# Turning the retrieved rows by VectorE and sixteen SBUF moves instead of by TensorE, and centring by VectorE

## Chip, cores and metric

The kernel runs on one core of a Trainium2 chip. The metric is the device time of one execution in microseconds (us), the median over several runs. Engines are called PE (TensorE), DVE (VectorE), ACT (ScalarE), POOL (GpSimd) and SP (SyncE, which here only issues DMAs).

## What is computed

The input has 2048 rows of 512 numbers. Each row is normalised; from it an attention retrieval over 8 selected heads of 128 and a dense layer with int8 weights are computed, and both are added to the row. The key and value projections only feed outputs that are dropped.

```python
xn = _layernorm(x, axis=-1)
q = xn @ Wq.T + bq                      # heads of 128; only heads 0, 4, 8, ... (8 of 32) are used
sig_q = jax.nn.elu(q) + 1.0
num = jnp.einsum('bshd,hde->bshe', q_sel, M)
den = jnp.einsum('bshd,hd->bsh', q_sel, z)[..., None] + EPS
retrieved = num / den                   # repeated for the 4 heads of a group
output = retrieved_heads @ Wo.T
dense = xn @ (w * w_scale) + b
x = x + output + dense
```

## The kernel before

The 2048 rows are 16 tiles of 128 (t = 0 to 15). M and Wo are folded once into a matrix P (8 pieces of 128x512, line 740), so that per tile three products are left: q = centred x times Wq (`product_q`, two halves of 512 columns, 24 matmuls), the dense product (`product_dense`, 12 matmuls) and a times P (`product_attn`, 24 matmuls). Each product is made of three passes over operands split into a high and a low part (`three_passes`, lines 677 to 679); so every operand exists as `_hi` (a rounding copy, mostly by ACT) and `_lo` (the rest, by DVE).

Per tile the way is: DVE takes the moments (lines 462, 466, 470). PE spreads the mean over the partitions with one transpose into `mean_ps` (line 687); ACT copies it to `mean_b` (line 324), and POOL subtracts it from the transposed tile `xT` (`center`, line 225); for tiles 0 and 1 DVE does this from `mean_ps` (lines 480, 487). ACT and DVE split `xT` (lines 339, 500). PE makes q in PSUM; DVE scales and adds the bias (`add_bias`, 531); ACT makes exp of the negative part (362, 364), DVE makes s = elu(q) + 1 (`make_s`, 538). POOL multiplies s by z (`times_z`, 256), DVE sums by head, adds the epsilon, takes the reciprocal (`denominator`, 543, 546, 550), ACT scales s by it, head by head, in place (`make_a`, 375): this is a, rows by heads. PE turns a with 8 transposes of 128x128 (`transpose_a`, 752) into two banks `aT_ps`; ACT and DVE split these into `aT_hi` and `aT_lo` (383, 563). Then `product_attn`, and DVE adds it to x (`add_attn`, 570; for the last tile line 671 in two halves).

The order of each engine is written out by hand; each engine works its list in order, and waits on semaphores. Tiles 0 to 6 are interleaved by hand with the loading of the weights and the making of P (by DMAs that POOL issues with addition, line 245, for the sum over the 4 head groups of Wo). Then a loop over t = 7 to 15 (LEAD = 7) does on PE: q(t), dense(t), spread of mean t+2, attn(t-7), turn of a(t-5). After the loop come attn(9) to attn(15) alone, with the remaining turns. DVE's body of the loop is: split of aT(t-6), bias, moments of t+2, bias, s, split of xT(t+1), s, dense added, denominator(t-4) (BEHIND = 4), attn(t-7) added. Eight PSUM banks: two for q, one dense, two aT, two attn, one mean; in tiles 0 to 6 q also uses the attn and aT banks. SP issues loads of x and xT, and the stores of finished tiles, each as one DMA of 128 partitions.

## Time and profile before

| | us |
|---|---|
| median of 3 runs | 260.02 |
| lowest, highest | 259.87, 264.77 |
| the profiled execution, its own time | 260.27 |
| its span in the trace (first to last instruction) | 258.5 |

The profile is one execution seen by the hardware profiler. The span leaves out what lies around the first and last instruction: 260.27 - 258.5 = 1.77 us. The granted TensorE clock is full in the whole span. A row that says "[1.21 <-DVE x L554]" means that the engine was idle 1.21 us before this instruction, until that line of DVE was done. Matmuls overlap in the rows: one takes 0.39 us from start to modelled end, but the next starts 0.23 us after it.

### The profile page before, as it was taken

Reading aid. Unit: us, or ns where it says so; the run is one execution under the profiler, and the core shown is the slowest. Engines: PE = TensorE matmul, PEld = TensorE weight load, DVE = VectorE, ACT = ScalarE, POOL = GpSimd, SP = SyncE. Lnnn points to the kernel's source line nnn. Section 1 sums busy time; section 2 is a strip of 40 time slices with the busy share of each in tenths; the row PEclk is TensorE's granted clock in tenths of the full one; section 3 lists DMA queues with packets and bytes.
Section 4 is the critical chain, followed back from the end, with each engine's and each line's share of the span. In section 5 each row is a group of like instructions: output and inputs, shape, how many; then the busy total and the mean of one; then the engine's idle time right before and its main releaser. Section 6 shows DMA issues by size and latency. Waiting matters only on the chain.

```text
span 258.5 us, 3387 instructions
## 1 busy us (share of the span) xinstructions
PE 249.9 (97%) x1156; PEld 201.2 (78%) x1156; DVE 156.2 (60%) x262; ACT 121.2 (47%) x276; POOL 103.2 (40%) x96
## 2 busy tenths in 40 slices
PE   6899899899998999999999999999999999999996
PEld 4477687687766888888888888888888888888885
DVE  4849996898677846457483746557463445555321
ACT  3653625657457554444345553544345345555100
POOL 2594745580303670705235070714305055563000
PEclk9999999999999999999999999999999999999999
DMA  7999999995400003030302103010101001111111
GB/s 247 414 411 406 345 228 218 209 217 153 146 16 4 0 13 109 0 124 1 122 1 66 58 0 122 3 41 0 41 3 41 1 1 43 41 41 43 49 49 64
DMA packets 9808, 26.42 MB, mean 102 GB/s; under 512 B 1088, under 2 KB 1344, under 8 KB 8640
## 3 DMA queue, kind: packets, MB, share of 16 engines
q1 hardware_dynamic: 8640, 19.40, 20.2%
q0 software_dynamic: 864, 6.29, 11.8%
q10 hardware_dynamic: 288, 0.52, 0.6%
q8 instruction: 9, 0.15, 0.2%
q14 instruction: 7, 0.06, 0.1%
HBM read 22.02 MB, written 4.19 MB: 101 GB/s over the span
## 4 chain that ended last, share of the span: by engine, by line
PE 84%; DVE 9%; ACT 2%; issue 2%; DMA 1%; DVEq 0%
PE attn_ps L679 11%; PE attn_ps L677 11%; PE attn_ps L678 11%; PE q_ps L677 8%; PE q_ps L679 8%; PE q_ps L678 8%; PE aT_ps L752 5%; PE dense_ps L677 5%; PE dense_ps L678 5%; PE dense_ps L679 5%; PE attn_ps L740 2%; DMA x<-in_x 1%; DVE stats L462 1%; DVE wd_lo L517 1%; DVE q_ps L531 1%
## 5 line engine op out<-in xcount | busy, mean ns | idle before, releaser
L256 POOL TENSOR_TENSOR e_and_sz<-s,z_b 128x512 f32<-128x512 f32 x32 | 41.7, 1330 | 31.4 <-DVE den L543 31.4
L375 ACT ACTIVATE s<-s,rden 128x128 f32<-128x128 f32 x128 | 39.2, 389 | 31.0 <-DVE rden L550 31.0
L677 PE MATMUL attn_ps<-P_hi,aT_hi 128*128 128x512 f32 (+1 forms) x128 | 50.2, 393 | 0.0
L679 PE MATMUL attn_ps<-P_hi,aT_lo 128*128 128x512 f32 (+1 forms) x128 | 49.2, 385 | 0.0
L678 PE MATMUL attn_ps<-P_lo,aT_hi 128*128 128x512 f32 (+1 forms) x128 | 49.0, 382 | 0.0
L570 DVE TENSOR_TENSOR x<-attn_ps,x 128x512 f32<-128x512 f32 x15 | 10.4, 691 | 46.4 <-PE attn_ps L679 46.4
L677 PE MATMUL q_ps<-WqT_hi,xT_hi 128*128 128x512 f32 x88 | 36.0, 409 | 0.6 <-DVE s L538 0.6
L679 PE MATMUL q_ps<-WqT_hi,xT_lo 128*128 128x512 f32 x88 | 34.4, 391 | 0.0
L678 PE MATMUL q_ps<-WqT_lo,xT_hi 128*128 128x512 f32 x88 | 34.3, 390 | 0.0
L219 POOL TENSOR_TENSOR rstd<-vareps,neg_half 128x1 f32<-128x1 f32 x16 | 10.6, 665 | 55.7 <-DVE vareps L470 55.7
L225 POOL TENSOR_TENSOR xT<-xT,mean_b 128x512 f32<-128x512 f32 x14 | 19.6, 1403 | 32.5 <-ACT mean_b L324 32.5
L531 DVE SCALAR_TENSOR_TENSOR q_ps<-q_ps,rstd,bq_b 128x512 f32<-128x512 f32 x24 | 18.1, 758 | 21.5 <-PE q_ps L679 21.5
L362 ACT ACTIVATE e_and_sz<-q_ps 128x512 f32<-128x512 f32 x24 | 14.3, 596 | 33.9 <-DVE q_ps L531 33.9
L679 PEld LDWEIGHTS attn_ps<-P_hi,aT_lo 128*128 128x128 f32 x128 | 24.1, 188 | 4.9
L677 PEld LDWEIGHTS attn_ps<-P_hi,aT_hi 128*128 128x128 f32 x128 | 24.1, 188 | 4.9
L678 PEld LDWEIGHTS attn_ps<-P_lo,aT_hi 128*128 128x128 f32 x128 | 24.1, 188 | 4.4
L677 PE MATMUL dense_ps<-wd_hi,xT_hi 128*128 128x512 f32 x64 | 25.6, 400 | 1.2 <-DVE x L554 1.2
L383 ACT ACTIVATE aT_hi<-aT_ps 128x512 fp32r<-128x512 f32 x32 | 17.4, 595 | 17.0 <-PE aT_ps L752 17.0
L679 PE MATMUL dense_ps<-wd_hi,xT_lo 128*128 128x512 f32 x64 | 24.9, 390 | 0.0
L678 PE MATMUL dense_ps<-wd_lo,xT_hi 128*128 128x512 f32 x64 | 24.9, 390 | 0.0
L563 DVE TENSOR_TENSOR aT_lo<-aT_ps,aT_hi 128x512 fp32r<-128x512 f32 x32 | 20.6, 685 | 5.2 <-ACT aT_hi L383 5.2
L364 ACT ACTIVATE e_and_sz<-e_and_sz 128x512 f32<-128x512 f32 x32 | 20.2, 632 | 1.0
(93 smaller groups left out, 407.9 us busy)
## 6 DMA issues: line engine op xcount, KB each, us to landing
x<-in_WoT POOLq DMA_DIRECT2D x6, 1024.0 KB, 9.6
x<-in_x SPq DMA_DIRECT2D x16, 256.0 KB, 3.7
xT<-in_xT SPq DMA_DIRECT2D x16, 256.0 KB, 4.1
out<-x SPq DMA_DIRECT2D x15, 256.0 KB, 2.0
x<-in_WoT SPq DMA_DIRECT2D x2, 1024.0 KB, 14.6
s<-in_WqT SPq DMA_DIRECT2D x3, 512.0 KB, 7.0
s<-in_w_scale SPq DMA_DIRECT2D x1, 1024.0 KB, 10.1
s<-in_WqT ACTq DMA_DIRECT2D x2, 256.0 KB, 4.2
```

The lines of the kernel that those rows point to most:

```text
L225: nc.gpsimd.tensor_tensor(xT[:, t % XRING, :, :], xT[:, t % XRING, :, :], mean_b[:, t % 2, :].unsqueeze(1).to_broadcast([P, K, P]), ALU.su ...
L256: nc.gpsimd.tensor_tensor(szbuf[:, halves(h)], sbuf_s[:, t % SRING, halves(h)], z_b[:, halves(h)], ALU.mult).then_inc(sz_ready, 1)
L362: nc.scalar.activation(e, q_bank(t, h)[:], ACT.Relu, scale=-1.0).then_inc(qneg_ready, 1)
L364: nc.scalar.activation(e, e, ACT.Exp, scale=-1.0).then_inc(exp_ready, 1)
L375: last = nc.scalar.activation(a_g, a_g, ACT.Copy, scale=rden[:, t % 2, g:g + 1])
L383: nc.scalar.activation(aT_hi[:, t % 2, h * GH:(h + 1) * GH, :].rearrange("p g r -> p (g r)"), aT_ps[h][:], ACT.Copy).then_inc(aT_hi_ready, 1)
L531: nc.vector.scalar_tensor_tensor(q_bank(t, h)[:], q_bank(t, h)[:], rstd[:, t:t + 1], bq_b[:, halves(h)], ALU.mult, ALU.add).then_inc(q_bia ...
L563: nc.vector.tensor_tensor(aT_lo[:, t % 2, gs, :].rearrange("p g r -> p (g r)"), aT_ps[h][:], aT_hi[:, t % 2, gs, :].rearrange("p g r -> p ...
L677: nc.tensor.matmul(out, x_hi, w_hi, start=start, stop=False)
L678: nc.tensor.matmul(out, x_hi, w_lo, start=False, stop=False)
L679: return nc.tensor.matmul(out, x_lo, w_hi, start=False, stop=stop)
L752: last = nc.tensor.transpose(aT_ps[h][:, i * P:(i + 1) * P], sbuf_s[:, t % SRING, g * D:(g + 1) * D], ident[:])
```

## The change

- PE no longer turns a. Instead DVE transposes the tile of a in place, in blocks of 32x32 (`turn_blocks`, one instruction on 128x1024), and SP moves the blocks with 16 DMAs of 32 partitions by 1 KB, SBUF to SBUF (`spread_blocks`), into `aT` for even tiles and into the space of `MT` (free once P is made) for odd ones. To make runs of 1 KB, the columns of Wq, bq and z are laid out by quarters of a head (32 columns of each head together); `times_z`, `make_a` and the splits read and write with views over four pieces of 32.
- DVE centres every tile from `mean_ps`; `copy_mean` on ACT and `center` on POOL are gone.
- The epsilon of the denominator is a 129th column that is summed with the others; the addition on DVE (line 546) is gone.
- The two banks of aT become a second pair of q banks; q(t) waits for s(t-2) instead of s(t-1).
- BEHIND is 3 instead of 4, the ring of s has 6 places instead of 7, and the lists of all engines are reordered to match. `spread_blocks(t)` waits for `turn_blocks(t)` and for the split of aT(t-2); `copy_aT_hi(t)` waits for all 16 DMAs; `make_s(t, 0)` waits for the DMAs of tile t-6.
- On PE 14 filling matmuls in bf16, 8 before and 6 after the first spread mean, replace 7 in fp32r and 5 in bf16; on SP the load of the second piece of Wq goes before that of x(1).

```diff
-    SRING = 7
+    SRING = 6
     XRING = 4
     HRING = 4
-    BEHIND = 4
+    BEHIND = 3
...
         sbuf_s = sb("s", [P, SRING, E])
-        e_and_sz = sb("e_and_sz", [P, 2, E])
+        aT = sb("aT", [P, 4, E // 4])
+        e_and_sz = sb("e_and_sz", [P, E + G * (D + 1)])
         aT_hi = sb("aT_hi", [P, 2, G, P], F32R)
         aT_lo = sb("aT_lo", [P, 2, G, P], F32R)
-        w_words = sb("w_words", [P, K, HID // 4], I32)
-        mean_b = sb("mean_b", [P, 2, P])
...
-        warm_b = sb("warm_b", [P, HID], BF16)
-
-        warm_r = P_hi[:, 0, :]
-        w_i8 = w_words[:].bitcast(I8)
+        warm = sb("warm", [P, P], BF16)
+
+        w_words = aT[:, 0:2, :].rearrange("p a (k w) -> p (a k) w", k=K // 2).bitcast(I32)
...
-        szbuf = e_and_sz[:, 1, :]
-        w_f32 = e_and_sz[:].rearrange("p r (a n) -> p (r a) n", n=HID)
+        ebuf = e_and_sz[:, 0:E]
+        sz_eps = e_and_sz[:, E:].rearrange("p (g d) -> p g d", g=G)
...
-        q_ps = [bank("q0_ps"), bank("q1_ps")]
+        q_ps = [bank(f"q{i}_ps") for i in range(4)]
         dense_ps = bank("dense_ps")
-        aT_ps = [bank("aT0_ps"), bank("aT1_ps")]
         attn_ps = [bank("attn0_ps"), bank("attn1_ps")]
         mean_ps = bank("mean_ps")
 
         def q_bank(t, h):
-            return ([q_ps, attn_ps, aT_ps][t % 3] if t < LEAD else q_ps)[h]
+            if t < LEAD and t % 3 == 1:
+                return attn_ps[h]
+            return q_ps[2 * (t % 3 == 2 if t < LEAD else t % 2) + h]
...
+        def by_quarter(v):
+            return v.rearrange("p (j g c) -> p j g c", g=G, c=D // 4)
+
+        def aT_place(t):
+            return [aT[:], MT[:].rearrange("p g d -> p (g d)").rearrange("p (i e) -> p i e", i=4)][t % 2]
+
+        def by_head(t, gs):
+            return aT_place(t).rearrange("p i (g r) -> p g i r", g=G)[:, gs]
+
+        def in_groups(v):
+            return v.rearrange("p g (i r) -> p g i r", i=4)
+
+        def aT_landed(t):
+            return 16 * 16 * (t // 2 + 1)
...
+            def spread_blocks(t):
+                sp.wait_ge(a_turned, t + 1)
+                if t == 1:
+                    sp.wait_ge(P_filled, G)
+                elif t >= 2:
+                    sp.wait_ge(aT_lo_ready, 2 * t - 2)
+                for i in range(4):
+                    for j in range(4):
+                        sp.dma_start(aT_place(t)[j * 32:(j + 1) * 32, i, :],
+                                     sbuf_s[i * 32:(i + 1) * 32, t % SRING, j * E // 4:(j + 1) * E // 4]
+                                     ).then_inc(aT_in[t % 2], 16)
...
-            for t in range(5, T):
-                if t >= FIRST_LENT:
-                    sp.wait_ge(P_filled, t - FIRST_LENT + 1)
+            for t in range(5, FIRST_LENT):
                 load_x(t)
                 load_xT(t)
-                if t >= 10:
-                    sp.wait_ge(attn_added, t - 9)
-                    sp.dma_start(out_d[t - 10], x[:, t - 10, :]).then_inc(stored, 16)
-            for t in range(T - 10, T - 1):
-                sp.wait_ge(attn_added, t + 1)
-                sp.dma_start(out_d[t], x[:, t, :]).then_inc(stored, 16)
+            spread_blocks(0)
+            for t in range(FIRST_LENT, LEAD + 4):
+                sp.wait_ge(P_filled, t - FIRST_LENT + 1)
+                load_x(t)
+                load_xT(t)
+            spread_blocks(1)
+            spread_blocks(2)
+            for t in range(LEAD, T):
+                if t + 4 < T:
+                    sp.wait_ge(P_filled, t + 4 - FIRST_LENT + 1)
+                    load_x(t + 4)
+                    load_xT(t + 4)
+                spread_blocks(t - BEHIND - 1)
+                if t - LEAD >= 1:
+                    store(t - LEAD - 1)
+            for t in range(T - BEHIND - 1, T):
+                spread_blocks(t)
+                store(t - BEHIND - 1)
+            for t in range(T - BEHIND - 1, T - 1):
+                store(t)
...
-            def center(t):
-                pool.wait_ge(mean_copied, t - 1)
-                pool.wait_ge(xT_in[t], 16)
-                nc.gpsimd.tensor_tensor(xT[:, t % XRING, :, :], xT[:, t % XRING, :, :],
-                                        mean_b[:, t % 2, :].unsqueeze(1).to_broadcast([P, K, P]), ALU.subtract
-                                        ).then_inc(xc_by_pool, 1)
...
-                nc.gpsimd.tensor_tensor(szbuf[:, halves(h)], sbuf_s[:, t % SRING, halves(h)],
-                                        z_b[:, halves(h)], ALU.mult).then_inc(sz_ready, 1)
+                nc.gpsimd.tensor_tensor(sz_eps[:, :, h * D // 2:(h + 1) * D // 2].rearrange("p g (j c) -> p j g c", j=2),
+                                        by_quarter(sbuf_s[:, t % SRING, halves(h)]), by_quarter(z_b[:, halves(h)]), ALU.mult
+                                        ).then_inc(sz_ready, 1)
...
-            def copy_mean(t):
-                act.wait_ge(mean_filled, t + 1)
-                if t >= 4:
-                    act.wait_ge(xc_by_pool, t - 3)
-                nc.scalar.activation(mean_b[:, t % 2, :], mean_ps[:, 0:P], ACT.Copy
-                                     ).then_inc(mean_copied, 1)
...
-                    a_g = sbuf_s[:, t % SRING, g * D:(g + 1) * D]
+                    a_g = by_quarter(sbuf_s[:, t % SRING, :])[:, :, g, :]
                     last = nc.scalar.activation(a_g, a_g, ACT.Copy, scale=rden[:, t % 2, g:g + 1])
                 last.then_inc(a_ready, 1)
 
             def copy_aT_hi(t):
+                act.wait_ge(aT_in[t % 2], aT_landed(t))
+                if t >= 2:
+                    act.wait_ge(attn_filled, t - 1)
                 for h in range(2):
-                    act.wait_ge(aT_filled, 2 * t + h + 1)
-                    if t >= 2:
-                        act.wait_ge(attn_filled, t - 1)
-                    nc.scalar.activation(aT_hi[:, t % 2, h * GH:(h + 1) * GH, :].rearrange("p g r -> p (g r)"),
-                                         aT_ps[h][:], ACT.Copy).then_inc(aT_hi_ready, 1)
+                    gs = slice(h * GH, (h + 1) * GH)
+                    nc.scalar.activation(in_groups(aT_hi[:, t % 2, gs, :]), by_head(t, gs), ACT.Copy).then_inc(aT_hi_ready, 1)
...
+            make_a(3)
             for t in range(LEAD, T):
-                copy_aT_hi(t - LEAD + 1)
                 exp_of(t, 0)
                 if t + 1 < T:
                     copy_xT_hi(t + 1)
                 exp_of(t, 1)
-                if t + 2 < T:
-                    copy_mean(t + 2)
+                copy_aT_hi(t - LEAD + 1)
                 make_a(t - BEHIND)
             for t in range(T - LEAD + 1, T):
                 copy_aT_hi(t)
-                if t + 2 < T:
-                    make_a(t + 2)
+                if t + BEHIND < T:
+                    make_a(t + BEHIND)
...
-            def center_second():
-                dve.wait_ge(mean_filled, 2)
-                dve.wait_ge(xT_in[1], 16)
-                nc.vector.tensor_tensor(xT[:, 1, :, :], xT[:, 1, :, :],
+            def center(t):
+                dve.wait_ge(mean_filled, t + 1)
+                dve.wait_ge(xT_in[t], 16)
+                nc.vector.tensor_tensor(xT[:, t % XRING, :, :], xT[:, t % XRING, :, :],
                                         mean_ps[:, 0:P].unsqueeze(1).to_broadcast([P, K, P]),
                                         ALU.subtract).then_inc(xc_by_dve, 1)
...
-                    dve.wait_ge(aT_filled, 2 * (t - SRING) + 2)
+                    dve.wait_ge(aT_in[(t - SRING) % 2], aT_landed(t - SRING))
...
-                nc.vector.reduce_sum(den[:], szbuf.rearrange("p (g d) -> p g d", g=G), AX.X
-                                     ).then_inc(den_ready, 1)
+                nc.vector.reduce_sum(den[:, t % 2, :], sz_eps, AX.X).then_inc(den_ready, 1)
                 dve.wait_ge(den_ready, t + 1)
-                nc.vector.tensor_scalar_add(den_e[:], den[:], DEN_EPS).then_inc(den_e_ready, 1)
-                dve.wait_ge(den_e_ready, t + 1)
                 if t >= 2:
                     dve.wait_ge(a_ready, t - 1)
-                nc.vector.reciprocal(rden[:, t % 2, :], den_e[:]).then_inc(rden_ready, 1)
+                nc.vector.reciprocal(rden[:, t % 2, :], den[:, t % 2, :]).then_inc(rden_ready, 1)
...
+            def turn_blocks(t):
+                dve.wait_ge(a_ready, t + 1)
+                nc.vector.transpose(sbuf_s[:, t % SRING, :], sbuf_s[:, t % SRING, :]).then_inc(a_turned, 1)
...
-                    nc.vector.tensor_tensor(aT_lo[:, t % 2, gs, :].rearrange("p g r -> p (g r)"), aT_ps[h][:],
-                                            aT_hi[:, t % 2, gs, :].rearrange("p g r -> p (g r)").bitcast(F32),
-                                            ALU.subtract).then_inc(aT_lo_ready, 1)
+                    nc.vector.tensor_tensor(in_groups(aT_lo[:, t % 2, gs, :]), by_head(t, gs),
+                                            in_groups(aT_hi[:, t % 2, gs, :]).bitcast(F32), ALU.subtract
+                                            ).then_inc(aT_lo_ready, 1)
...
+            center(3)
...
+            center(8)
+            turn_blocks(2)
             for t in range(LEAD, T):
-                split_aT_lo(t - LEAD + 1)
                 add_bias(t, 0)
                 if t + 2 < T:
                     moments(t + 2)
                 add_bias(t, 1)
+                turn_blocks(t - BEHIND - 1)
                 make_s(t, 0)
                 if t + 1 < T:
                     split_xT_lo(t + 1)
                 make_s(t, 1)
+                split_aT_lo(t - LEAD + 1)
                 add_dense(t)
+                if t + 2 < T:
+                    center(t + 2)
                 denominator(t - BEHIND)
+                if t == T - 1:
+                    denominator(T - BEHIND)
                 add_attn(t - LEAD)
             for t in range(T - LEAD, T - 1):
                 split_aT_lo(t + 1)
-                if t + 3 < T:
-                    denominator(t + 3)
+                if t + BEHIND < T:
+                    turn_blocks(t + BEHIND)
+                if t + BEHIND + 2 < T:
+                    denominator(t + BEHIND + 2)
                 add_attn(t)
             for c in range(2):
...
-                if 1 <= t <= 2:
+                if t >= 1:
                     pe.wait_ge(xc_by_dve, t + 1)
-                elif t >= 3:
-                    pe.wait_ge(mean_copied, t - 2)
...
-                    pe.wait_ge(s_ready, 2 * (t - 3 if t < LEAD else t - 1) + h + 1)
+                    pe.wait_ge(s_ready, 2 * (t - 3 if t < LEAD else t - 2) + h + 1)
...
-            def transpose_a(t):
-                pe.wait_ge(a_ready, t + 1)
-                for h in range(2):
-                    if t == 0:
-                        pe.wait_ge(s_ready, 11 + h)
-                    else:
-                        pe.wait_ge(aT_lo_ready, 2 * t - 1 + h)
-                    for i in range(GH):
-                        g = h * GH + i
-                        last = nc.tensor.transpose(aT_ps[h][:, i * P:(i + 1) * P],
-                                                   sbuf_s[:, t % SRING, g * D:(g + 1) * D], ident[:])
-                    last.then_inc(aT_filled, 1)
...
-            pe.wait_ge(warm_set, 2)
-            for i in range(3):
-                nc.tensor.matmul(dense_ps[:], warm_r[:, 0:P], warm_r, start=True, stop=True)
-            for i in range(4):
-                nc.tensor.matmul(aT_ps[i % 2][:], warm_r[:, 0:P], warm_r, start=True, stop=True)
+            def keep_busy(n):
+                for i in range(n):
+                    nc.tensor.matmul(dense_ps[:], warm[:], warm[:].unsqueeze(1).to_broadcast([P, 4, P]), start=True, stop=True)
+
+            pe.wait_ge(warm_set, 1)
+            keep_busy(8)
             pe.wait_ge(consts_set, 3)
             spread_mean(0)
-            for i in range(5):
-                nc.tensor.matmul(dense_ps[:], warm_b[:, 0:P], warm_b[:], start=True, stop=True)
+            keep_busy(6)
...
-            transpose_a(0)
...
-                transpose_a(t - LEAD + 2)
             for t in range(T - LEAD, T - 1):
                 product_attn(t)
-                if t + 2 < T:
-                    transpose_a(t + 2)
```

## Rows read from the trace of the kernel before

**Rows 1.** The page: each engine's busy time, share of the span, instructions.
```profile
PE 249.9 (97%) x1156; PEld 201.2 (78%) x1156; DVE 156.2 (60%) x262; ACT 121.2 (47%) x276; POOL 103.2 (40%) x96
```

**Rows 2.** The page: the chain that ended last, shares by engine.
```profile
PE 84%; DVE 9%; ACT 2%; issue 2%; DMA 1%; DVEq 0%
```

**Rows 3.** Chain in order of time: start us, us, what; end of P, turns.
```profile
75.04 0.87 PE attn_ps L740 x2
...
75.94 0.61 ACT P_hi L368
...
76.56 0.69 DVE P_lo L522
77.26 1.19 DVE aT_lo L563 x2
...
79.19 1.10 PE attn_ps L740 x2
80.29 0.87 PE aT_ps L752 x8
...
81.28 0.23 PE q_ps L677
...
212.05 0.88 PE aT_ps L752 x8
```

**Rows 4.** Timeline of PE and ACT, tiles 2 to 5: start, us, what, idle before.
```profile
31.12 0.47 PE L677 MATMUL q_ps<-WqT_hi,xT_hi 128*128 128x512 f32 x1 [0.55 <-DVE s L538]
...
46.37 0.50 PE L677 MATMUL dense_ps<-wd_hi,xT_hi 128*128 128x512 f32 x1 [1.21 <-DVE x L554]
...
39.72 0.28 ACT L324 ACTIVATE mean_b<-mean_ps 128x128 f32<-128x128 f32 x1 [5.66 <-PE mean_ps L687]
```

**Rows 5.** Groups by line: busy us, mean ns of one, idle before.
```profile
L543 DVE TENSOR_REDUCE den<-e_and_sz 128x8 f32<-128x1024 f32 x16 | 19.3, 1209 | 0.0
L546 DVE TENSOR_SCALAR den_e<-den 128x8 f32<-128x8 f32 x16 | 5.8, 361 | 0.6
L487 DVE TENSOR_TENSOR xT<-xT,mean_ps 128x512 f32<-128x512 f32 x1 | 0.7, 675 | 0.0
L517 DVE TENSOR_TENSOR wd_lo<-s,wd_hi 128x1024 fp32r<-128x1024 f32 x2 | 3.4, 1762 | 0.0
```

**Rows 6.** Stretches of one loop pass: busy us by engine, clock, DMA share, GB/s.
```profile
110.60:125.20 14.60, 14.60 (x71) 12.10 (x70) 8.49 (x15) 6.75 (x17) 5.63 (x5) 1.00 0.17 56
```

**Rows 7.** Timelines of SP's queue: start us, us, issue.
```profile
2.12 0.43 SPq L170 DMA_DIRECT2D s<-in_WqT  x1
2.59 0.43 SPq L167 DMA_DIRECT2D xT<-in_xT  x1
...
15.60 2.34 SPq L162 DMA_DIRECT2D x<-in_x  x1
...
61.31 0.33 SPq L162 DMA_DIRECT2D x<-in_x  x1
61.68 0.43 SPq L167 DMA_DIRECT2D xT<-in_xT  x1
```

**Rows 8.** DMA issues: KB each, us from issue to landing.
```profile
out<-x SPq DMA_DIRECT2D x15, 256.0 KB, 2.0
out<-x SPq DMA_DIRECT2D x2, 128.0 KB, 1.7
```

**Rows 9.** Timelines of DVE and POOL: subtraction alone, and beside POOL's product.
```profile
12.52 0.69 DVE L500 TENSOR_TENSOR xT_lo<-xT,xT_hi 128x512 fp32r<-128x512 f32 x1
...
18.70 2.53 DVE L500 TENSOR_TENSOR xT_lo<-xT,xT_hi 128x512 fp32r<-128x512 f32 x1 [3.77 <-ACT xT_hi L339]
...
18.29 2.39 POOL L237 TENSOR_TENSOR s<-e_and_sz,s 128x1024 f32<-128x1024 f32 x1 [0.43 <-ACT e_and_sz L349]
```

**Rows 10.** Timelines of the last loop pass and the end: ACT, DVE, POOL.
```profile
205.35 0.63 ACT L364 ACTIVATE e_and_sz<-e_and_sz 128x512 f32<-128x512 f32 x1
...
212.53 1.09 ACT L383 ACTIVATE aT_hi<-aT_ps 128x512 fp32r<-128x512 f32 x2 [0.85 <-PE aT_ps L752]
...
213.16 1.29 DVE L563 TENSOR_TENSOR aT_lo<-aT_ps,aT_hi 128x512 fp32r<-128x512 f32 x2 [0.38 <-ACT aT_hi L383]
...
250.18 0.69 DVE L570 TENSOR_TENSOR x<-attn_ps,x 128x512 f32<-128x512 f32 x1 [3.97 <-PE attn_ps L679]
...
208.60 2.54 POOL L256 TENSOR_TENSOR e_and_sz<-s,z_b 128x512 f32<-128x512 f32 x2 [10.71 <-DVE den L543]
```

More of the change, by code:

```diff
@@ L143, in retrieval_and_dense @@
         dense_added = sem("dense_added")
-        aT_filled = sem("aT_filled")
+        a_turned = sem("a_turned")
+        aT_in = [sem(f"aT_in{i}") for i in range(2)]
         aT_hi_ready = sem("aT_hi_ready")
@@ L248, in times_z @@
             def times_z(t, h):
-                if t == 0 and h == 0:
+                if t == 0:
                     pool.wait_ge(z_in, 16)
-                if t == 0:
-                    pool.wait_ge(wd_by_pool, 1)
+                    pool.wait_ge(eps_set, 1)
                 else:
@@ L313, in _ @@
                 times_z(t, 1)
-                add_b(t - BEHIND + 2)
-            for t in range(T - 2, T):
+                add_b(t - 3)
+            for t in range(T - 3, T):
                 add_b(t)
@@ L621, in _ @@
             add_bias(4, 1)
+            center(6)
             denominator(1)
+            turn_blocks(0)
             make_s(4, 0)
@@ L639, in _ @@
             split_P_lo(3)
+            denominator(3)
             split_xT_lo(7)
@@ L876 @@
         "xT": tiles.reshape(16, 128, 4, 128).transpose(0, 3, 2, 1).reshape(16, 128, 512),
-        "WqT": np.asarray(inputs["L0_attn_Wq"]).reshape(8, 4, 128, 4, 128).transpose(1, 3, 4, 0, 2).reshape(
+        "WqT": np.asarray(inputs["L0_attn_Wq"]).reshape(8, 4, 4, 32, 4, 128).transpose(1, 4, 5, 2, 0, 3).reshape(
             4, 4, 128, 1024),
-        "bq": np.asarray(inputs["L0_attn_bq"]).reshape(8, 4, 128)[:, 0].reshape(1024),
+        "bq": np.asarray(inputs["L0_attn_bq"]).reshape(8, 4, 4, 32)[:, 0].transpose(1, 0, 2).reshape(1024),
         "WoT": np.asarray(inputs["L0_attn_Wo"]).reshape(512, 2, 4, 4, 128).transpose(3, 1, 4, 2, 0).reshape(
@@ L882 @@
         "MT": np.asarray(inputs["L0_attn_M"]).transpose(2, 0, 1),
-        "z": np.asarray(inputs["L0_attn_z"]),
+        "z": np.asarray(inputs["L0_attn_z"]).reshape(8, 4, 32).transpose(1, 0, 2).reshape(1024),
         "w": np.ascontiguousarray(np.asarray(inputs["L0_ffn_w"]).reshape(4, 128, 512).transpose(1, 0, 2)).view(np.int32),
```

62 lines of the change are left out of this document (25 added, 37 removed).

## The prediction

> **What bounds the kernel now.** I read four views in this order. The page's first part: PE is busy in 97% of the span, DVE in 60, ACT in 47, POOL in 40 [rows 1]; the clock is full in the loop [rows 6]. The chain that ended last says the same more strictly: 84% of it is PE [rows 2]. Then the chain in order of time, for what PE does in a tile: the 8 turns of a stand in it with 0.88 us [rows 3], 16 times. So a microsecond taken from PE's list is worth a microsecond, as long as no other engine's list becomes the longer. Last, the timelines of tiles 2 to 6 and of the end, where PE does wait: 0.55 us for s at 31.12, 1.21 us for the dense sum at 46.37 [rows 4]. A loop pass from q to attn is 13.6 us without turns: from 81.28 to 212.05 there are nine passes and eight turns, (130.8 - 7.0) / 9 = 13.75 with the spread mean in most [rows 3].
>
> **PE loses the turns.** 16 x 0.87 = 13.9 us of list. The first two stand in the stretch where P is made. There a chain of product, copy 0.61, subtraction 0.69, split of aT(0) 1.19, subtraction, last product and the moments of tile 8 goes on without them. From the product at 75.04 to q of tile 7 at 81.28 it is 6.24 us; by that chain about 5.6 remain, a gain of 0.6 in place of 1.7 [rows 3]. The other 14 give 12.2.
>
> **Centring moves to DVE.** ACT loses the copy of the mean, POOL a product-sized instruction, DVE gets 0.68 per tile [rows 5], 14 tiles. In the loop DVE is busy 8.49 of 14.60 us [rows 6]; that becomes 8.5 + 0.7 + 1.2 (turn, below) - 0.2 = 10.2 of 13.7. Hidden. In tiles 2 to 5 DVE itself is on the chain, so each added 0.68 could cost. But there ACT stood 5.66 us in front of the mean of tile 5 [rows 4] with the exp of tile 2 behind it in its list, and two subtractions ran against POOL (1.76 us each where 1.2 is the size of a reduction over as many elements [rows 5]). Both go. Walking DVE's new list through, s(0) comes about 1.0 us earlier, so q of tile 3 starts about 0.9 earlier and dense of tile 1 about 0.8; the exp of tile 2 no longer waits, and add_dense(2) ends near 43.5 where PE comes to dense(3) at 44.3 instead of 46.37. I take 2.1 us gained; if the added work eats it, 0; these are the bounds.
>
> **The epsilon column.** The addition averages 361 ns where the reciprocal beside it is shorter, since it gets caught behind POOL [rows 5]. Gone, off PE's path: no term of its own. Two more q banks relax a wait that cost PE nothing in the loop: nothing. The new filling on PE ends about 0.4 us later before the first q, where PE then waits for weights anyway: nothing, up to 0.5 lost.
>
> **DVE's turn of 128x1024.** No row shows it. Nearest is the reduction over 128x1024, 1.21 us [rows 5]; as a lower bound 0.7, as an upper one twice the reduction, 2.4. I take 1.2. The Trainium skill ("VectorE: DVE Perf Modes", The three transpose paths) gives 311 ns for a 128x128 bf16 turn of this kind, which for eight would be an estimate of 2.5 us and put the sum below 1.3 us higher.
>
> **SP's sixteen moves per tile** are the term that takes back. DMAs issued in a row on SP start 0.47 us apart (2.12, 2.59), whatever their size; the shortest is 0.33, 0.37 to the next (61.31, 61.68) [rows 7]. Landing is 1.7 to 2.0 us after the issue [rows 8]. I take 0.47 and 2.0: a tile is 7.5 us of issue, plus a store. In the loop that is 19 issues, 8.9 of 13.7 us. spread_blocks(t) holds behind it on SP the next loads, needed two passes later, and a store; copy_aT_hi, which waits for the landing, comes a pass later; make_s(7, 0), which waits for tile 1's moves (they must wait for the end of P), may hold DVE a microsecond where PE has five in hand. So the loop runs on PE.
>
> At the end it doesn't. Call E the end of attn(8); attn(9) to attn(15) take 5.48 us each without turns (from 212.05 + 0.88 to 250.18, six products and five turns [rows 3, 10]), so attn(15) could start at E + 32.9. SP has four tiles of moves and three stores before it. In the last pass tile 11's moves wait for the split of aT(9), which now stands behind s(15, 1): by [rows 10] the exp ends 7.6 us into the pass, the split near 9.9, that is E - 3.7. Moves of 11 and a store end at E + 4.3. Tile 12's wait for its turn: DVE has before it denominator(13), which needs POOL's product of 2.54 us started behind denominator(12), then add_attn(8) and the split of aT(10). This gives E + 5.3. The split now has both inputs in SBUF; such a subtraction took 0.69 alone and 2.53 beside POOL [rows 9], so up to E + 7.1; I take E + 6. The last issue starts 66 issues later (4 x 16 + 3 stores, less one), lands after 2.0, half a copy and half a split (0.55 and 0.7 [rows 10]) follow: attn(15) at E + 6 + 66 x 0.47 + 2.0 + 1.25 = E + 40.3. Stall 7.4 us, spread over attn(13) to attn(15).
>
> **Sum.** E was at 212.05; less 2.1, 0.6 and 8 loop turns of 0.87 (7.0) it is 202.35. Plus 40.3, plus 8.3 from attn(15) to the end of the span (250.18 to 258.5), plus 1.77 outside it: 252.7 us against 260.27 of the profiled execution. The median is 0.25 under that: 252.4.
>
> **The rivals.**
> 1. *The moves are issued faster.* At 0.37 apart and a turn at E + 5.3 the stall is gone: 202.35 + 32.9 + 8.3 + 1.77 = 245.3, 245.1 as a median. For it: the shortest issue; against it: 0.43 and 0.47 in every row of several issues [rows 7].
> 2. *The end costs more or the start gives nothing.* With no early gain (+2.1), the split of aT(10) fully behind POOL (+1.1) and a slow turn (+1.2): 256.8. Each tenth of a microsecond on the issue is 6.6 us, so 0.53 apart gives 256.4 alone.
> 3. *Slower: small moves hold the queue.* If each DMA holds SP as long as one did with a full queue, 2.34 us [rows 7], 19 per pass are 44 us and the kernel is beyond 500. It decides from 0.59 apart (the sum passes 260.3) and from 13.7 / 19 = 0.72 SP bounds the loop as well; at 0.8 nine passes of 15.2 add another 13 us to the end's 22: about 288. For it: the long issues exist; against it: they lie where the DMA engines are full, and in the loop their share is 0.17 [rows 6]. The Trainium skill ("DMA: Bandwidth & Descriptors", Bandwidth) warns that transfers under 64 KB are dominated by descriptors and asks for 1 MiB or more; these have 32 KB. No row of before shows one of that size.
> 4. *DVE becomes the bound*: it needs a turn of 1.2 + (13.7 - 10.2) = 4.7 us, four times the reduction.
>
> **How the numbers follow.** My forecast 0.50 (its own range 249.5 to 254.8), rival 1 with all between 0.37 and 0.43 apart 0.22, rival 2 0.18, rival 3 0.07, rival 4 0.03. The predicted time is 252.4. The range reaches down to rival 1 and up past rival 2: 245.0 to 258.5. About 2% is what a measurement here can tell from no change: under 254.8 is faster, over 265.2 slower. The forecast lies under that line in nine of ten of its cases, rival 1 always, a tenth of rival 2: 0.45 + 0.22 + 0.02 = 0.69. Slower takes most of rivals 3 and 4: 0.08. The rest is 0.23.
>
> **What would show it.** DVE's turn near 1.2 us; SP's moves 0.47 apart, and 256 of them; no idle on PE in the loop, a pass of 13.7 us; dense(3) starting near 44; then PE waiting for the split of aT in front of attn(13), attn(14) and attn(15), about 7 us together, with SP's queue never idle from E on. If PE doesn't wait there, the moves are cheaper than I take them; if it waits inside the loop, they or the turn are dearer. What makes the forecast wrong first is the price of an issue, the factor 66 in the sum.

## The result and the profile after

The kernel after takes 277.9 us (median of 4 runs, 276.06 to 278.19) where the kernel before takes 260.0: a ratio of 1.0675, interval 1.0617 to 1.0733. The forecast was 252.4, with 245.0 to 258.5 as its range. It is slower, outside the range and on the other side. The profiled execution is 278.12 us with a span of 276.5.

The page of after: each engine's busy time, the granted clock over the span in 40 slices, and the chain that ended last by engine and by line.

```profile
PE 247.3 (89%) x1030; PEld 193.0 (70%) x1030; DVE 178.7 (65%) x275; ACT 117.9 (43%) x262; POOL 86.3 (31%) x83
...
PEclk9999995799999999999999999999999998959959
...
PE 58%; SPq 22%; DMA 10%; DVE 4%; issue 4%; ACT 1%
SPq L197 17%; DMA x<-in_x 9%; PE q_ps L708 8%; PE q_ps L706 8%; PE q_ps L707 8%; PE attn_ps L706 7%; PE attn_ps L707 7%; PE attn_ps L708 7%; PE dense_ps L706 4%; PE dense_ps L708 4%; PE dense_ps L707 4%; PE attn_ps L767 2%; SPq L180 1%; SPq L175 1%; DVE s L549 1%
```

Beside [rows 1] PE lost 126 instructions but only 2.6 us of busy time, because the clock is no longer full: it falls in two places, near 50 us and in the last fifth. Beside [rows 2] PE's share of the chain falls from 84 to 58%. Two newcomers took its place: SP issuing the moves (L197) and one load of x. PE's waits, summed by line (total us, times, longest), give each newcomer a size.

```profile
PE attn_ps L706 <- DVE aT_lo L575: 14.1, 4, 5.4
PE dense_ps L706 <- DVE x L562: 5.1, 1, 5.1
```

**The start.** q of tile 7 begins at 88.86 where it was 81.28 [rows 3]: 7.6 us lost. The chain in order of time (start, us, what) shows why:

```profile
13.46 25.97 DMA x<-in_x
...
39.46 0.70 DVE stats L473
```

PE's timeline has the wait that comes of it, and the windows (columns as in [rows 6]) what the clock was afterwards:

```profile
45.82 0.80 PE L706 MATMUL dense_ps<-wd_hi,xT_hi 128*128 128x512 f32 x1 [5.08 <-DVE x L562]
```
```profile
45.80:51.70 5.90, 5.88 (x14) 4.63 (x15) 5.04 (x10) 4.16 (x9) 1.83 (x3) 0.50 1.04 215
```

x of tile 5 is issued at 13.46 and lands at 39.43. DVE stands 6.3 us in front of its moments, everything behind them on DVE stands too, PE waits 5.1 us for the dense sum, and then runs 5.9 us at a granted clock of 0.50, the lower of its two levels. What changed around this load is on POOL: the adding transfers of Wo start 5 us earlier. POOL's timeline of before:

```profile
24.84 2.18 POOL L225 TENSOR_TENSOR xT<-xT,mean_b 128x512 f32<-128x512 f32 x1 [0.84 <-ACT mean_b L324]
26.98 1.92 POOL L245 DMA_DIRECT2D x<-in_WoT  x2
```

And that of after:

```profile
21.52 0.55 POOL L259 TENSOR_TENSOR rstd<-vareps,neg_half 128x1 f32<-128x1 f32 x1 [3.21 <-DVE vareps L481]
22.02 1.02 POOL L278 DMA_DIRECT2D x<-in_WoT  x1
23.57 0.86 POOL L278 DMA_DIRECT2D x<-in_WoT  x1 [0.53 <-DMA x<-in_WoT]
```

The centring of tile 3 used to stand in front of them in POOL's list: with its wait it took 3.0 us there (from 24.0 to 27.0). It is gone. The other 1.9 us are DVE's: POOL's instruction before it, which needs the moments of tile 3, starts at 21.52 where it started at 23.46, since DVE reaches these moments at 20.35 instead of 22.29. Together these move the transfers forward by 5.0 us. What they do to the DMA engines is in the windows of after (last two columns: DMA share, GB/s):

```profile
22.00:26.00 4.00, 4.00 (x19) 3.25 (x19) 2.64 (x5) 1.57 (x3) 1.91 (x3) 1.00 1.02 394
26.00:30.00 4.00, 3.73 (x17) 2.77 (x16) 3.93 (x8) 1.77 (x4) 0.52 (x1) 1.00 1.10 254
```

The windows of before have the same fall, only later:

```profile
26.00:30.00 4.00, 3.94 (x18) 2.92 (x16) 3.98 (x4) 2.86 (x5) 2.90 (x3) 1.00 1.04 386
30.00:34.00 4.00, 3.20 (x14) 2.52 (x15) 3.96 (x8) 3.14 (x6) 1.82 (x2) 1.00 1.07 242
```

**The loop** is as forecast. A pass, from q of tile 7 on, is 13.8 us, and PE never stops in it:

```profile
88.80:102.60 13.80, 13.80 (x62) 11.25 (x61) 8.38 (x14) 7.44 (x18) 4.84 (x5) 1.00 0.19 49
```

attn(8) ends at E = 212.6, where it ended at 212.05 before: the start's 7.6 us have eaten the eight turns.

**The end** takes 63.9 us from E to the end of the span; before it was 46.45 (212.05 to 258.5). The chain of after, from the second of tile 11's moves to the split in front of attn(15):

```profile
210.14 0.59 SPq L197
210.77 0.59 SPq L197
...
262.00 0.59 SPq L197
262.63 1.84 DMA MT<-s
264.49 0.64 ACT aT_hi L403
265.15 0.70 DVE aT_lo L575
```

SP's timeline has tile 12's sixteen moves:

```profile
220.32 10.06 SPq L197 DMA_DIRECT2D aT<-s  x16
```

PE's timeline, its waits in front of attn(12) to attn(15):

```profile
233.14 0.76 PE L706 MATMUL attn_ps<-P_hi,aT_hi 128*128 128x512 f32 x1 [2.82 <-DVE aT_lo L575]
...
243.88 0.77 PE L706 MATMUL attn_ps<-P_hi,aT_hi 128*128 128x512 f32 x1 [3.58 <-DVE aT_lo L575]
...
254.66 0.47 PE L706 MATMUL attn_ps<-P_hi,aT_hi 128*128 128x512 f32 x1 [2.29 <-DVE aT_lo L575]
...
265.90 0.58 PE L706 MATMUL attn_ps<-P_hi,aT_hi 128*128 128x256 f32 x1 [5.40 <-DVE aT_lo L575]
```

The windows there, with the clock in the third column from the end:

```profile
225.00:245.00 20.00, 13.60 (x50) 10.36 (x49) 7.73 (x11) 4.64 (x12) 4.63 (x4) 0.86 0.26 75
266.00:276.50 10.50, 7.75 (x48) 7.54 (x48) 1.90 (x4) 0.00 (x0) 0.00 (x0) 0.80 0.18 65
```

SP's queue is the chain without a gap, and an issue follows the other after 0.63 us, not 0.47. The clock is low for a part of these stretches (0.86 and 0.80 on average), where it was full before, and what follows attn(15)'s start takes 10.6 us instead of 8.3.

So the balance of 18.0 us of span: +7.6 at the start, -7.0 for the loop's turns, +17.4 at the end.

### The profile page after: what moved, and what is told of

Its sections match the earlier page's. It is cut to its first block, busy times and chain, and to the rows that moved or that the text cites. A ratio compares the mean times of both kernels' runs of the same rounds, so it can differ in the third digit from the quotient of the medians.

```text
span 276.5 us, 3351 instructions
## 1 busy us (share of the span) xinstructions
PE 247.3 (89%) x1030; PEld 193.0 (70%) x1030; DVE 178.7 (65%) x275; ACT 117.9 (43%) x262; POOL 86.3 (31%) x83
## 3 DMA queue, kind: packets, MB, share of 16 engines
HBM read 22.02 MB, written 4.19 MB: 95 GB/s over the span
## 4 chain that ended last, share of the span: by engine, by line
PE 58%; SPq 22%; DMA 10%; DVE 4%; issue 4%; ACT 1%
SPq L197 17%; DMA x<-in_x 9%; PE q_ps L708 8%; PE q_ps L706 8%; PE q_ps L707 8%; PE attn_ps L706 7%; PE attn_ps L707 7%; PE attn_ps L708 7%; PE dense_ps L706 4%; PE dense_ps L708 4%; PE dense_ps L707 4%; PE attn_ps L767 2%; SPq L180 1%; SPq L175 1%; DVE s L549 1%
## 5 line engine op out<-in xcount | busy, mean ns | idle before, releaser
L706 PE MATMUL attn_ps<-P_hi,aT_hi 128*128 128x512 f32 (+1 forms) x128 | 53.4, 417 | 14.1 <-DVE aT_lo L575 14.1
L707 PE MATMUL attn_ps<-P_lo,aT_hi 128*128 128x512 f32 (+1 forms) x128 | 52.0, 406 | 0.0
L706 PE MATMUL q_ps<-WqT_hi,xT_hi 128*128 128x512 f32 x104 | 41.7, 401 | 0.4 <-DVE s L549 0.4
L708 PE MATMUL q_ps<-WqT_hi,xT_lo 128*128 128x512 f32 x104 | 40.6, 390 | 0.0
L707 PE MATMUL q_ps<-WqT_lo,xT_hi 128*128 128x512 f32 x104 | 40.5, 389 | 0.0
L706 PEld LDWEIGHTS q_ps<-WqT_hi,xT_hi 128*128 128x128 f32 x104 | 19.5, 187 | 5.3 <-issue 1.2
L575 DVE TENSOR_TENSOR aT_lo<-MT,aT_hi 128x512 fp32r<-128x512 f32 x16 | 11.9, 785 | 17.1 <-ACT aT_hi L403 17.1
L707 PEld LDWEIGHTS q_ps<-WqT_lo,xT_hi 128*128 128x128 f32 x104 | 19.6, 188 | 4.5 <-issue 0.5
L708 PEld LDWEIGHTS q_ps<-WqT_hi,xT_lo 128*128 128x128 f32 x104 | 19.5, 188 | 4.2
L549 DVE SCALAR_TENSOR_TENSOR s<-q_ps,e_and_sz 128x512 f32<-128x512 f32 x28 | 18.7, 675 | 4.9 <-DMA MT<-s 3.8
## 6 DMA issues: line engine op xcount, KB each, us to landing
x<-in_x SPq DMA_DIRECT2D x16, 256.0 KB, 3.9
xT<-in_xT SPq DMA_DIRECT2D x16, 256.0 KB, 4.6
out<-x SPq DMA_DIRECT2D x15, 256.0 KB, 2.3
x<-in_WoT SPq DMA_DIRECT2D x2, 1024.0 KB, 14.1
```

The lines of the kernel that those rows point to most:

```text
L549: nc.vector.scalar_tensor_tensor(sbuf_s[:, t % SRING, halves(h)], q_bank(t, h)[:], 0.0, ebuf[:, halves(h)], ALU.max, ALU.add).then_inc(s_r ...
L575: nc.vector.tensor_tensor(in_groups(aT_lo[:, t % 2, gs, :]), by_head(t, gs), in_groups(aT_hi[:, t % 2, gs, :]).bitcast(F32), ALU.subtract) ...
L706: nc.tensor.matmul(out, x_hi, w_hi, start=start, stop=False)
L707: nc.tensor.matmul(out, x_hi, w_lo, start=False, stop=False)
L708: return nc.tensor.matmul(out, x_lo, w_hi, start=False, stop=stop)
```

## The experiments

Two causes were to be told apart from their rivals: for the start, that the earlier adding transfers delay x(5); for the end, the price of an issue. All ratios are to the kernel before on the same chip.

**POOL waits for x(5) before it adds.**

```diff
+            pool.wait_ge(x_in[5], 16)
             add_wo(1, 0)
```

> The changed kernel, with one wait more: POOL issues the first adding transfer of Wo only when x(5) has landed. Theory A: x(5) came at 39.46 us since POOL, rid of centring, issues its two adding transfers of 1 MB at 22.0 and 23.6 us instead of 27.0, in front of loads still under way. Then x(5) lands before 32 us, DVE's wait of 6.3 us is gone, the TensorE clock stays full at 46 us, dense of tile 3 starts near 44, q of tile 7 at about 80 instead of 88.9, and the time is near 268.5 us. Rival B: the load of z (now one run of 4 KB per partition instead of 8 of 512 B) or the new order of SP's loads delays x(5): then nothing moves, 277.9 us.

Measured: 270.38 us (269.12 to 271.67), ratio 1.0325, interval 1.0240 to 1.0409; 1.9 us more than theory A expected. The adding transfers start at 30.16, and DVE goes through tile 5's moments without a wait (POOL's timeline, then DVE's):

```profile
30.16 1.93 POOL L278 DMA_DIRECT2D x<-in_WoT  x2 [7.20 <-DMA x<-in_x]
```
```profile
33.36 0.74 DVE L563 SCALAR_TENSOR_TENSOR x<-dense_ps,rstd,x 128x512 f32<-128x512 f32 x1
34.02 0.68 DVE L474 BATCH_NORM_STATS2 stats<-x 128x6 f32<-128x512 f32 x1
```

q of tile 7 is back at 81.3 (80 expected). One wait added to a DMA queue brings 7 us, and the cause of the start's loss is shown: the early adding transfers. x of tile 5 has landed by 30.16. The dense product of tile 3 begins at 45.34 (46.37 before [rows 4]), so of the early gain about half appears. In this execution it does not last: PE stands 1.0 us in front of P's first product (PE's timeline). The row doesn't name what it waited for; that it is the sum of Wo, whose adding transfers were held back, is my reading and not shown.

```profile
60.27 1.10 PE L768 MATMUL attn_ps<-x,MT 128*128 128x512 f32 x2 [1.01 <-issue]
```

In other executions it does last. The three kernels under "What sets the price of an issue" differ from this one only from tile 0's moves on, at 54.8 us (the third only from tile 1's), and there the product begins between 59.02 and 59.35, and q of tile 7 at 79.8 to 80.2 in PE's timeline, where before has 81.0. So with this wait the start gives between 0 and 1.2 us.

**z loaded as runs of 512 bytes.** The rival for the start was that the load of z, whose layout was changed, crowds x(5) out.

```diff
-            sp.dma_start(z_b[:], z_d.unsqueeze(0).to_broadcast([P, E])).then_inc(z_in, 16)
+            sp.dma_start(z_b[:].rearrange("p (g d) -> p g d", g=G),
+                         z_d.rearrange("(g d) -> g d", g=G).unsqueeze(0).to_broadcast([P, G, D])).then_inc(z_in, 16)
```

> The changed kernel with z loaded in eight runs of 512 B per partition, as before the change. Theory A (adding transfers issued too early): no change, x(5) lands near 39, 277.9 us. Rival B (the load of z): x(5) lands before 32 us, about 268.5 us.

Measured: 273.55 us in one execution, between what the two theories expected. The wait for x(5) shrinks to 2.2 us and PE's to 2.7. But the adding transfers also start 1.0 us later here than in after, at 23.03, because DVE reaches the moments of tile 3 at 21.36 instead of 20.35. It does so without any edit of z as well, at 21.24 in the kernel with POOL's wait. So what the load's shape has to do with the 4 us stays open. It isn't needed to explain the loss, as the next two show.

**The centring alone, on the kernel before, without and with the wait.** DVE centres all tiles, `copy_mean` and `center` on POOL go; nothing else of the change is there, z's load included.

```diff
-                nc.gpsimd.tensor_tensor(xT[:, t % XRING, :, :], xT[:, t % XRING, :, :],
-                                        mean_b[:, t % 2, :].unsqueeze(1).to_broadcast([P, K, P]), ALU.subtract
-                                        ).then_inc(xc_by_pool, 1)
+                nc.vector.tensor_tensor(xT[:, t % XRING, :, :], xT[:, t % XRING, :, :],
+                                        mean_ps[:, 0:P].unsqueeze(1).to_broadcast([P, K, P]),
+                                        ALU.subtract).then_inc(xc_by_dve, 1)
```

> The kernel before with DVE's centring alone (ACT's copy of the mean and POOL's subtraction gone, DVE's list as in the change); SP's loads, the layouts and PE's turns stay as before. Theory: the early loss of the change comes from this part, since POOL then issues the adding transfers of Wo at 22 to 24 us: x(5) lands near 39 us, DVE waits for it some 6 us, time near 267 us. Rival: the load of z in one run and the new order of SP's loads, which this kernel does not have, make x(5) late: then x(5) lands before 33 us and the time is 258 to 260 us.

> The same with POOL's first adding transfer held until x(5) has landed. Theory: DVE's list from 20 to 47 us runs as walked through in the prediction, dense of tile 3 starts near 44 instead of 46.4, but the first product of P still waits for the sum of Wo until about 60.3 us (as in the changed kernel with this wait), so that next to nothing is left: 259 to 260 us. If the sum of Wo did not hold P, 258.

Measured: alone 267.41 us, ratio 1.0251 (1.0180 to 1.0322); with the wait for x(5) 259.15 us, ratio 0.9932 (0.9885 to 0.9979). The timelines of POOL and of DVE in the kernel with the centring alone have the same two rows as after:

```profile
21.82 1.02 POOL L236 DMA_DIRECT2D x<-in_WoT  x1
```
```profile
39.17 0.69 DVE L426 BATCH_NORM_STATS2 stats<-x 128x6 f32<-128x512 f32 x1 [6.20 <-DMA x<-in_x]
```

So the start's loss belongs to the centring part of the change. DVE's 14 added instructions cost nothing: with the wait, P's first product starts at 59.23 (60.26 before) and q of tile 7 1.0 us earlier than before. What costs is that POOL comes to its DMA issues sooner. With the order restored the part is worth about 1 us (the interval leaves 0.5 to 3), less than the 2% from which a change counts as one here.

**PE turns the last four tiles, without and with POOL's wait.** For tiles 12 to 15 PE turns a into two banks of q that are free by then; SP's moves and DVE's turns stop at tile 11, and ACT puts the columns of these tiles back in the order of heads. The lines that matter most:

```diff
+                if t >= BY_PE:                       # BY_PE = 12
+                    return copy_aT_hi_ps(t)
...
                 product_attn(t)
+                if BY_PE <= t + 2 < T:
+                    transpose_a(t + 2)
```

> The changed kernel with tiles 12 to 15 turned by PE into the free second pair of q banks, no DMA moves for them. Theory: the end is bound by SP, which issues a move each 0.63 us (10.8 us per tile with its store, against 5.5 us per attn product); then PE's waits of 2.8, 3.6, 2.3 and 5.4 us and the halved clock behind them are gone, from the end of attn(8) (212.6 us) to the end of the span it takes 46.45 - 0.87 - 0.87 = 44.7 us instead of 63.9, the time is about 259. Rival: DVE's splits beside POOL (2.9 us instead of 1.3 at 216 and 222 us) or denominator(13) ahead of add_attn(8) hold the end: then PE still waits before attn(10) to attn(12) and the time stays above 265.

> Both edits together (POOL waits for x(5); tiles 12 to 15 turned by PE). If the two losses are separate, the gains add: 277.9 - 9.4 - 18.9 = about 249.6 us, 4% under the kernel before. If the start's loss only hides behind something else (the sum of Wo arriving later, so that P starts no earlier), about 259.

Measured: without POOL's wait 260.08 us (median of 10 runs; nine between 259.19 and 261.0, one at 252.91, which is the time of the kernel with the wait). The traced one of the nine has the same 6.4 us of DVE waiting for x(5). Whether x(5) came in time in the tenth no trace shows; its mean granted clock was 1.00 where the nine had 0.98 to 0.99, which fits. With it 252.92 us (252.04 to 253.08), ratio 0.9651, interval 0.9580 to 0.9721; repeated later on another chip 252.72, ratio 0.9654. PE has no wait for aT_lo left and the clock is full in all 40 slices. This version is faster than both kernels. The 249.6 expected from adding the gains added forecasts of 9.4 and 18.9; measured, the two edits alone gave 7.5 and 17.8, and together 25.0, so they do add. That 252.9 is close to the 252.4 forecast for the change is luck: it is another kernel. Its turns on PE, in PE's timeline, are like this one:

```profile
216.97 1.03 PE L806 MATMUL q_ps<-ident,s 128*128 128x128 f32 x8
```

A turn of a tile stands in the chain with 0.87 us (217.13 to 218.00), so four of them put back 3.5 us of the 12.2 that the loop and the end had to give.

**What sets the price of an issue.** Three kernels, each with POOL's wait, change the move alone, and each leaves out a part of the computation (the blocks are not rearranged, or not moved, or only in part): one takes all 128 partitions with 256 bytes each, one reads 32 partitions by 1 KB from x in HBM, one cuts the moves of odd tiles to 128 bytes per partition.

```diff
-                        sp.dma_start(aT_place(t)[j * 32:(j + 1) * 32, i, :],
-                                     sbuf_s[i * 32:(i + 1) * 32, t % SRING, j * E // 4:(j + 1) * E // 4]
# wide, cols = slice(j * 64, (j + 1) * 64)
+                        sp.dma_start(aT_place(t)[:, i, cols],
+                                     sbuf_s[:, t % SRING, i * E // 4 + j * 64:i * E // 4 + (j + 1) * 64]
# from HBM
+                        sp.dma_start(aT_place(t)[j * 32:(j + 1) * 32, i, :],
+                                     x_d[t][i * 32:(i + 1) * 32, 0:E // 4]
# narrow (n = 32 for odd t)
+                        sp.dma_start(aT_place(t)[j * 32:(j + 1) * 32, i, 0:n],
+                                     sbuf_s[i * 32:(i + 1) * 32, t % SRING, j * E // 4:j * E // 4 + n]
```

> The changed kernel with the wait for x(5), its 16 moves per tile made as 128 partitions by 256 B, SBUF to SBUF, same bytes (the blocks are not rearranged: this part of the computation is left out). It asks what a move's 0.63 us on SP are made of, against 0.47 us of a load. If the 32 partitions cost it, an issue here is 0.47 us; if having both ends in SBUF costs it, it stays 0.63. The end follows: at 0.47, attn(15) starts 84 x 0.16 = 13 us earlier and the time is about 258; at 0.63 about 270.

> The changed kernel with the wait for x(5), its 16 moves per tile reading 32 partitions by 1 KB from the input x in HBM instead of from s in SBUF (the turned data are not moved: left out). If both ends in SBUF cost the 0.63 us, an issue here is 0.47 us and the time about 258 us; if the 32 partitions cost it, 0.63 and about 270 us.

> The kernel after with POOL's wait for x(5), and with the moves of odd tiles cut from 1 KB to 128 bytes per partition (columns beyond the first 32 of each piece are not moved, so the attention sum of odd tiles is built on stale data: part of the computation is left out). Theory that the time of an issue depends on where the two ends are and not on how many bytes a move has: SP's issues of odd tiles stand 0.60 long and 0.64 apart, exactly like those of even tiles, and the end has the same waits of PE in front of attn(12) to attn(15), 14 us together; time near 270. Rival, that the issue grows with the bytes: the issues of odd tiles are shorter (0.45 or less) and two of four tiles at the end save 16 x 0.2 us each, time near 265.

Measured: wide 270.04, from HBM 256.01, narrow 270.02 us, one execution each. SP's timeline (start, us of all sixteen, issue) of the wide kernel:

```profile
211.63 10.30 SPq L198 DMA_DIRECT2D aT<-s  x16
```

Of the kernel that reads from HBM:

```profile
211.16 7.27 SPq L197 DMA_DIRECT2D aT<-in_x  x16
```

Of the narrow one, a tile of 128-byte runs and behind it one of 1 KB:

```profile
201.10 10.01 SPq L198 DMA_DIRECT2D MT<-s  x16
...
211.83 10.02 SPq L198 DMA_DIRECT2D aT<-s  x16
```

10.01 and 10.02 us with an eighth of the bytes and with all of them: size doesn't enter. Nor does the number of partitions, 10.30 with 128 of them. With the source in HBM it is 7.27, 0.46 apart, the price taken from [rows 7]. A store has its source in SBUF and a load its target, and neither costs this. What remains is that source and target both lie in SBUF. And the price falls on whatever is issued next: in after the first DMA behind a group of moves is mostly a store of x to HBM, and it takes 0.58, the load behind it 0.43; where a load of x comes first (74.53 and 109.20) it is the load that takes 0.58. SP's timeline of after:

```profile
134.55 10.05 SPq L197 DMA_DIRECT2D MT<-s  x16
144.64 0.58 SPq L203 DMA_DIRECT2D out<-x  x1
145.26 0.43 SPq L175 DMA_DIRECT2D x<-in_x  x1
```

In the kernel before, where no move stands ahead, such a store takes 0.34:

```profile
139.81 0.34 SPq L205 DMA_DIRECT2D out<-x  x1
```

**The list of DVE while P is made.** The best version starts q of tile 7 at 81.3, as before, though two turns of PE are gone from that stretch. To see whether DVE's list holds it, two entries are moved.

```diff
             split_P_lo(3)
-            denominator(3)
...
             split_P_lo(4)
+            moments(8)
             split_aT_lo(0)
             split_P_lo(5)
             split_P_lo(6)
-            moments(8)
+            denominator(3)
             split_P_lo(7)
```

> The kernel of run both (PE turns the last four tiles, POOL waits for x(5)) with DVE's list changed in the stretch where P is made: the moments of tile 8 stand right behind the split of P's fifth piece instead of behind the seventh, and denominator(3) stands behind the seventh instead of in front of the fifth. Theory that this stretch runs on DVE's list: the chain from the first product of P to q of tile 7 loses the denominator's 1.2 to 1.4 us and the moments' 0.7 behind the last product; q of tile 7 starts 1 to 2 us earlier than 81.3, time 251.0 to 252.0 where both has 252.9. Rival, that PE and ACT with the arrival of the summed Wo set it: q of tile 7 stays at 81.3 within 0.4 and the time at 252.9 within 0.4.

> The same kernel as run both, on the chip of p_order and in the same rounds, so that the two can be set against each other: 252.9 within 0.5, ratio to before 0.965 to 0.972, q of tile 7 at 81.3.

Measured in the same rounds: 253.39 us (251.71 to 254.2) against 252.72 (251.46 to 255.73), with ratios to before of 0.9673 (0.9609 to 0.9738) and 0.9654 (0.9593 to 0.9715): no gain, and the expected 1 us is missed. PE's timeline of the reordered kernel:

```profile
79.70 2.05 PE L794 MATMUL attn_ps<-x,MT 128*128 128x512 f32 x2 [1.71 <-DVE P_lo L552]
```

And of the other:

```profile
77.77 1.10 PE L794 MATMUL attn_ps<-x,MT 128*128 128x512 f32 x2 [0.82 <-DVE P_lo L552]
79.57 1.10 PE L794 MATMUL attn_ps<-x,MT 128*128 128x512 f32 x2 [0.70 <-DVE P_lo L552]
...
81.09 0.32 PE L741 MATMUL mean_ps<-ident,meanvar 128*128 128x128 f32 x1 [0.43 <-DVE meanvar L496]
```

The moments no longer stand behind the last product, but now they stand in front of the splits that release it, so the last product starts no earlier. In this execution two waits of 0.82 and 0.70 us have become 0.65 and 1.71, after which the product takes 2.05 instead of 1.10 us, at a mean clock of 0.81 from 77 to 81. From P's first product to q of tile 7 it is 21.9 us instead of 20.8. The traced execution took 254.2 us, the longest of six; four of the six, at 251.71 to 253.42, had a full clock throughout, so the fall of the clock isn't in all of them. DVE is busy nearly without a gap there in both (3.93 and 3.86 of the 4 us from 77 to 81). That its whole list, not the place of one entry, holds this stretch is what the rows suggest; a kernel with less DVE work in it wasn't run.

## Why the prediction was wrong

**PE loses the turns: right.** The loop gave its 7.0 us, in passes of 13.8 (forecast 13.75), with no wait.

**Gain of 0.6 in the stretch of P: wrong.** The walk took the turns out of the chain and left DVE's list as it was. In the kernel with POOL's wait it is 20.8 us in PE's timeline from the first product of P to q of tile 7 (60.27 to 81.07), and before it was 20.8 too (60.26 to 81.03). The chain of the kernel with POOL's wait shows what it went through in place of PE's turns, five instructions of DVE in a row between two products of P:

```profile
73.62 1.23 DVE den L555
74.99 0.65 DVE xT_lo L512
75.64 0.66 DVE x L563
76.30 0.60 DVE s L550
76.90 0.61 DVE P_lo L534
```

The forecast's chain had none of the first four. Whether DVE's own turn of tile 1, which lies in this stretch too (66.23 in the best version), has a part in it no run tells.

**Centring: the step that failed first.** "DVE gets 0.68 per tile ... Hidden" held: the instruction takes 672 to 689 ns, and PE has no wait in the loop. But the sentence that POOL loses "a product-sized instruction" stopped at the gain. It never asked what stands behind `center(3)` in POOL's list. There stand DMA issues, which move up with it (26.98 to 22.02) into a stretch where the DMA engines are full, and a load that DVE needs lands at 39.4 instead of in time. Where the bounds were 2.1 us gained and 0, and 0.6 more were counted for the stretch of P, q of tile 7 comes 7.6 us later. It was readable: POOL's timeline of before has `center` and the issues next to each other, and its windows show 386 GB/s falling to 242 when these transfers run. When an engine off the path starts its transfers was asked of SP's queue and not of POOL's.

**Without that loss the early gain arrives in part.** With POOL's wait dense(3) came 1.0 us earlier, not 2.1, and q of tile 7 between 0 and 1.2 us earlier, depending on the execution. That is inside the bounds named, nearer to the lower one.

**DVE's turn: right.** 1.2 was taken from the reduction's size; it is 1.233, 16 times:

```profile
L567 DVE STREAM_TRANSPOSE s<-s 128x1024 f32<-128x1024 f32 x16 | 19.7, 1233 | 0.0
```

The Trainium skill ("VectorE: DVE Perf Modes", The three transpose paths) gives 311 ns for a 128x128 turn in bf16, which gives an estimate of 2.5 us for eight of that size; the trace shows half, in float32. The row of the nearest instruction was the better source.

**SP's moves: the mis-sized term.** The price of an issue was taken as 0.47, and it is 0.63. The rest of this sum held: the last issue starts 66 issues after tile 12's first (220.32 to 262.63, 42.3 us, which is 66 x 0.633 and one issue at 256.30 that took 0.6 longer), lands in 1.84 (2.0 taken), and attn(15) starts 3.3 us after it (3.25). So attn(15) comes at E + 53.3 instead of E + 40.3: 42.3 instead of 31.0, or 11.3 us, for the issues, and 1.7 because tile 12's first move starts at E + 7.7, not E + 6. That too is mostly the price: SP was still busy with tile 11, whose moves and store took 10.7 us instead of 8.0. PE stands in front of attn(12) as well, and waits 14.1 us in all where three waits of together 7.4 were forecast. On top comes a term that the sum didn't have: after waits of 2 to 5 us PE starts at the lower clock, and the last stretch costs 2.3 us more. 13.0 + 2.3 make 15.3 us, and with the start's 10.3 (7.6 and the 2.7 that didn't come) 25.6 us of span. The profiled execution missed its 252.7 by 25.4.

With the issue at 0.46, as in the kernel that reads from HBM, the forecast's sum without early gain, 252.7 + 2.7 = 255.4, stands against 256.0 measured. There attn(15) starts 41.2 us after the end of attn(8) (40.3 in the sum), and PE waits 5.2 us in three places (7.4 taken); the clock averages 0.94 from 214 to 244, so a part of the agreement is that two errors cancel. The mechanism of the end was right, its unit price was not.

**The rivals.** Rival 3 named the point from which the sum passes the kernel before, 0.59 apart, and the truth is beyond it. But its mechanism, small transfers that hold the queue, isn't the cause: 128 bytes per partition cost the same as 1 KB, and the loop stays on PE (its own limit was 0.72). The rule of the Trainium skill named there ("DMA: Bandwidth & Descriptors", Bandwidth) says that a transfer this small pays for its descriptors rather than its bytes. The trace agrees in that a move of 32 KB lands after 1.8 us where a store of 256 KB took 2.0 [rows 8]; the loss here was in the issues on the queue, not in that. Rival 2's upper step, 0.53, was too small a margin: the bound on the price came from rows of DMAs between HBM and SBUF, and no row of before had one within SBUF. A term with a factor of 66 and no row of its own kind deserved a wider range than any other. Rival 4 was rightly small. So the chance of 0.08 for slower was too small for two independent reasons: the start's 10.3 us alone would have put the time at 262.7, the end's 15.3 alone at 267.7.

**DVE beside POOL: right.** The split of aT with both inputs in SBUF takes 2.90 us for two halves while POOL works, 1.29 otherwise. The Trainium skill ("SBUF — State Buffer", Who interferes with whom) says that a DVE instruction with two SBUF inputs contends with a GpSimd instruction that reads SBUF. The trace agrees: POOL's products of s and z, both in SBUF, run from 221.16 to 224.16, beside this row.

```profile
221.81 2.91 DVE L575 TENSOR_TENSOR aT_lo<-MT,aT_hi 128x512 fp32r<-128x512 f32 x2
```

## What to carry to other kernels

When an instruction is taken from an engine, read what stands behind it in that engine's list, DMA issues first: an engine that is idle half the time can still be what keeps a transfer from starting too early, and one explicit wait restores the order. A term that is multiplied by dozens (issues in a row on one queue) needs a row of exactly its own kind, with the same ends, and where none exists its bounds belong in the range with the full factor. Moves that hide in a loop come out in the tail, where nothing covers them; hand the last tiles to the engine that has become free there.

## What was not expected of the hardware

- DMAs issued in a row on SP stand 0.63 us apart when both ends are in SBUF, with 128 or 1024 bytes per partition and on 32 or 128 partitions, and 0.46 to 0.47 when one is in HBM. That holds in the loop and at the end; while POOL's adding transfers ran, sixteen moves took 12.8 us instead of 10.0 (from 54.84 in the kernel with POOL's wait). The DMA behind such a move takes 0.58 on the queue, be it a store (else 0.34 to 0.42) or a load (else 0.43).
- When the adding transfers of POOL's queue run, the 16 DMA engines stay fully busy and move 254 GB/s in place of 394, and a load of 256 KB issued on SP 8.6 us before them landed 26.0 us after its issue. With them held back, q of tile 7 came 7.6 us earlier.
- In the traced execution of the reordered kernel PE waited 1.7 us in one piece while P was made, and the granted clock averaged 0.81 over the 4 us around it; in that of the other, with waits of 0.8 and 0.7 us in the same place, it stayed at 1.00. Four of the six executions of the reordered kernel kept a full clock, so one such wait doesn't always lower it.
